# Two graph layers, second layer: an eighth unit by seven products, and two `lo` parts kept in DRAM

## What is computed

```python
def _L0_gnn_ref(h, adj, W_neigh, b_neigh, W_self, b_self):
    deg = jnp.sum(adj, axis=1, keepdims=True) + 1e-05
    h_neigh = (adj / deg) @ h
    out = h_neigh @ W_neigh.T + b_neigh + h @ W_self.T + b_self
    return jax.nn.relu(out)

def _L1_gnn_ref(x, adj, W, b):
    rowsum = adj.sum(axis=1)
    d_inv_sqrt = jnp.where(rowsum > 0, rowsum ** (-0.5), 0.0)
    support = (d_inv_sqrt[:, None] * adj * d_inv_sqrt[None, :]) @ x
    return jax.nn.relu(support @ W + b)
...
x = _layernorm(x + _L0_gnn_ref(x, adj, ...), axis=-1)
x = _layernorm(x + _L1_gnn_ref(x, adj, L1_gnn_W, L1_gnn_b), axis=-1)
```

## Time and profile before

| | us |
|---|---|
| median of 3 runs (lowest, highest) | 776.36 (775.98, 776.51) |
| profiled execution | 776.1 |
| its span, first to last instruction | 774.4 |
| TensorE busy in it | 766.6 |
| VectorE busy | 720.0 |
| ScalarE busy | 429.5 |
| moved by transfers | 161.09 MB |

### The profile page before, as it was taken

The page is one execution under the profiler, slowest core; times in us unless marked ns, Lnnn a source line. Parts: engine busy times, 40 slices in busy tenths (PEclk is TensorE's granted clock), DMA queues, the critical chain, the costliest instruction groups (busy, mean ns, idle before and its releaser), DMA issues.

```text
span 774.4 us, 12666 instructions
## 1 busy us (share of the span) xinstructions
PE 766.6 (99%) x4151; PEld 662.6 (86%) x4151; DVE 720.0 (93%) x1226; ACT 429.5 (55%) x594; POOL 2.5 (0%) x14
## 2 busy tenths in 40 slices
PE   9999999999999999999999999999999999999996
PEld 6888888888888888888888889899898989989896
DVE  6999999999899899998989899898989989898996
ACT  5644645646446364454554755665565566656663
POOL 0000000000000000000000000000000000000000
PEclk9999999999999999999999999999999999999999
DMA  7975574655646547474574756656565665756651
GB/s 302 346 237 195 191 264 155 243 187 200 234 154 244 189 168 266 135 267 168 176 260 147 243 178 208 216 195 241 172 228 198 215 217 176 257 165 229 204 190 61
DMA packets 54206, 161.09 MB, mean 208 GB/s; under 512 B 5024, under 2 KB 18080, under 8 KB 54176
## 3 DMA queue, kind: packets, MB, share of 16 engines
q1 hardware_dynamic: 45680, 151.54, 55.9%
q10 hardware_dynamic: 8352, 9.05, 3.7%
q0 software_dynamic: 144, 0.13, 0.2%
HBM read 152.31 MB, written 8.39 MB: 208 GB/s over the span
## 4 chain that ended last, share of the span: by engine, by line
PE 98%; DVE 1%; ACT 1%; issue 0%; ACTq 0%
PE ps_main L1100 72%; PE ps_epi L979 7%; PE ps_epi L1047 7%; PE ps_main L1038 4%; PE ps_main L1047 2%; PE ps_epi L1038 2%; PE ps_main L979 1%; PE ps_main L1075 1%; PE ps_main L1122 1%; PE ps_main L1060 1%; PE ps_epi L1132 0%; ACT hi L359 0%; ACT xt_sb L382 0%; ACT tt L406 0%; DVE tt L618 0%; PE ps_epi L1000 0%
## 5 line engine op out<-in xcount | busy, mean ns | idle before, releaser
L359 ACT ACTIVATE hi<-raw 128x1024 fp32r<-128x1024 f32 x254 | 254.9, 1013 | 134.5 <-PE ps_main L1100 86.9
L562 DVE TENSOR_TENSOR lo<-raw,hi 128x1024 fp32r<-128x1024 f32 x254 | 296.7, 1170 | 22.5 <-ACT hi L359 22.0
L1100 PE MATMUL ps_main<-hi,xs 128*128 128x512 f32 x1120 | 278.8, 391 | 0.0
L1100 PEld LDWEIGHTS ps_main<-hi,xs 128*128 128x128 f32 x1120 | 207.4, 188 | 41.7 <-issue 0.5
L1100 PE MATMUL ps_main<-lo,xs 128*128 128x512 f32 x560 | 149.7, 389 | 0.0
L853 DVE TENSOR_TENSOR acc<-acc,raw 128x1024 f32<-128x1024 f32 x112 | 136.4, 1218 | 0.0
L1100 PE MATMUL ps_main<-hi,zs 128*128 128x512 f32 x504 | 125.6, 391 | 0.0
L1100 PEld LDWEIGHTS ps_main<-lo,xs 128*128 128x128 f32 x560 | 105.1, 188 | 21.9
L1100 PEld LDWEIGHTS ps_main<-hi,zs 128*128 128x128 f32 x504 | 92.2, 188 | 17.6
L359 ACT ACTIVATE xs<-acc 128x1024 fp32r<-128x1024 f32 (+1 forms) x52 | 54.6, 1050 | 69.3 <-DVE acc L746 55.8
L1047 PE MATMUL ps_epi<-xs 128*128 128x256 f32 x423 | 69.7, 283 | 0.0
(11 more groups left out here) (158 smaller groups left out, 814.8 us busy)
## 6 DMA issues: line engine op xcount, KB each, us to landing
raw<-adj_t SPq DMA_DIRECT2D x256, 512.0 KB, 3.3
res<-x_nat SPq DMA_DIRECT2D x11, 512.0 KB, 5.3
xt_sb<-xt SPq DMA_DIRECT2D x8, 512.0 KB, 5.1
x_scratch<-tt ACTq DMA_DIRECT2D x8, 512.0 KB, 3.8
res<-x_scratch SPq DMA_DIRECT2D x8, 512.0 KB, 4.8
out<-tt ACTq DMA_DIRECT2D x7, 512.0 KB, 4.9
tt<-x_nat SPq DMA_DIRECT2D x3, 512.0 KB, 4.7
acc<-x_nat ACTq DMA_DIRECT2D x1, 512.0 KB, 5.0
```

The lines of the kernel that those rows point to most:

```text
L359: return act.activation(dst, src, ACT.Copy)
L562: return dve.tensor_tensor(dst, src, hi_part.bitcast(f32), ALU.subtract)
L1100: last = pe.matmul(ps[:, f, :], stationary(layer, part, jt, f), mov[:, slot(u), cols], start=(jt == 0 and i == 0), stop=(jt == JT - 1 and ...
```

## The change

- `SU` gets unit 4, so that blocks 1 to 6 of the second layer have eight units by seven products. The last block keeps the five it had, now in a tuple of its own, `SU_LAST`.
- A unit's place in the rings is counted in its own block's list (`s_place`). The table of t sums grows by two tiles of `xs`, and the third place of the ring moves out of `xs` into the first layer's weights `wn` and `ws`, which the loop of the second layer has no use for.
- The t sums of the last group are now those of two units (12 and 13), as in the other groups.
- First layer, blocks 1 to 6: behind the `adj` loads of units 10 and 14, SP stores `lo` of units 6 and 10 (512 KB each, 12 stores in all). VectorE waits for the store before it writes that slot of `lo` again.
- Second layer, blocks 1 to 6: behind the `adj` loads of units 9 and 13, SP waits for `h_ready` of units 6 and 10 and loads their `lo` from DRAM. TensorE's third pass waits for that load. VectorE does a memset of one column in place of `lo`, which gives the signal that frees `raw`.

```diff
@@ -40,9 +40,12 @@
-SU = (1, 5, 7, 9, 11, 12, 13)
+SU = (1, 4, 5, 7, 9, 11, 12, 13)
+SU_LAST = (1, 5, 7, 9, 11)
 NS = len(SU)
 SRING = 3
+KEPT = (6, 10)
+NK = len(KEPT)
 T_AT = XC + FH
 T_UNITS = (4, 6, 9, 11)
 S_AT = T_AT + 2 * NS
...
+        lo_dram = nc.dram_tensor("lo_scratch", [NB, NK, P, UW], f32, kind="Internal").ap()
...
+        lo_stored = [sem(f"lo_stored{s}") for s in range(RING)]
+        lo_full = [sem(f"lo_full{s}") for s in range(RING)]
...
@@ -192,7 +198,28 @@
                 return ()
-            return tuple(u for u in SU if u < TAIL) if is_last(b) else SU
+            return SU_LAST if is_last(b) else SU
+        def kept(b):
+            return () if isinstance(b, int) else KEPT
+        def kept_in_slot(u):
+            return [v for v in KEPT if slot(v) == slot(u)]
+        def kept_count(b, u):
+            per_block = len(kept_in_slot(u))
+            return (b * per_block + (kept_in_slot(u).index(u) + 1 - per_block)) * 16
+        def lead(v):
+            return 1 if v == 2 else max(v - 2, 0)
+        def s_place(b, u):
+            return by_seven(1, b).index(u)
...
@@ -208,19 +235,22 @@
-            return b * NS + (SU.index(u) - NS)
-            return acc[:, (SU.index(u) + 1 - parity) % 2, :]
-            at = S_AT + SU.index(u) % SRING * 4 + part * 2
+            return b * NS + (s_place(b, u) - NS)
...
+            return acc[:, (s_place(b, u) + NS * (1 - parity)) % 2, :]
...
+            s = s_place(b, u) % SRING
+            if s == SRING - 1:
+                return (wn, ws)[part][:, :, :, :].rearrange("p a k f -> p (a k f)")
+            at = S_AT + s * 4 + part * 2
             return xs[:, at:at + 2].rearrange("p a c f -> p (a c f)")
@@ -301,6 +331,17 @@
                     sp.dma_start(raw[:, slot(u), :], adj_in[b, u]).then_inc(raw_full[slot(u)], 16)
+                    if layer == 0 and u - RING in kept(b):
+                        sp.dma_start(lo_dram[b, KEPT.index(u - RING)], lo[:, slot(u), :].bitcast(f32))\
+                          .then_inc(lo_stored[slot(u)], 16)
+                    if layer == 1 and is_first(b) and u == NU - 1:
+                        for v in KEPT:
+                            sp.wait_ge(lo_stored[slot(v)], len(kept_in_slot(v)) * (NB - 2) * 16)
+                    if layer == 1 and u - RING + 1 in kept(b):
+                        v = u - RING + 1
+                        sp.wait_ge(h_ready, g0 + (v + 1))
+                        sp.dma_start(lo[:, slot(v), :].bitcast(f32), lo_dram[b, KEPT.index(v)])\
+                          .then_inc(lo_full[slot(v)], 16)
...
@@ -732,8 +773,8 @@
-                s1, s2, s3 = [s_sum(parity, u, i) for i in range(3)]
-                if SU.index(u) >= 2:
+                s1, s2, s3 = [s_sum(b, parity, u, i) for i in range(3)]
+                if s_place(b, u) >= 2:
                     dve.wait_ge(sl_ready, g - 1)
...
@@ -821,11 +862,18 @@
                         dve.wait_ge(h_ready, g0 + (u + 1))
                         cols = slice(0, UW - HB if u in by_seven(layer, b) else UW)
-                        split_lo(lo[:, slot(u), cols], raw[:, slot(u), cols], hi[:, slot(u), cols]).then_inc(l_ready, 1)
+                        if layer == 0 and u - RING in kept(b):
+                            dve.wait_ge(lo_stored[slot(u)], kept_count(b, u - RING))
+                        if layer == 1 and u in kept(b):
+                            dve.memset(marks[:, 2:3], 0.0).then_inc(l_ready, 1)
+                        else:
+                            split_lo(lo[:, slot(u), cols], raw[:, slot(u), cols], hi[:, slot(u), cols])\
+                                .then_inc(l_ready, 1)
                     place(u, 1)
                     if by_seven(layer, b):
-                        ahead = [v for v in by_seven(layer, b) if max(v - 2, 0) == u]
-                        slot_taken = u in SU and u + 1 in SU
+                        units = by_seven(layer, b)
+                        ahead = [v for v in units if lead(v) == u]
+                        slot_taken = ahead and len([v for v in units if u <= v < ahead[0]]) == 2
                         if ahead and not slot_taken:
                             s_sums(b, parity, ahead[0])
                         if u in by_seven(layer, b):
...
@@ -1092,7 +1140,9 @@
-                        if i == 2:
+                        if i == 2 and layer == 1 and u in kept(b):
+                            pe.wait_ge(lo_full[slot(u)], kept_count(b, u))
+                        elif i == 2:
                             pe.wait_ge(l_ready, g0 + (u + 1))
```

More of the change, by code:

```diff
@@ L209, in s_index, with s_sums_of, s_sum, s_part @@
         def s_index(b, u):
-            return b * NS + (SU.index(u) - NS)
-        def s_sums_of(parity, u):
-            return acc[:, (SU.index(u) + 1 - parity) % 2, :]
-        def s_sum(parity, u, i):
-            return s_sums_of(parity, u)[:, i * HB:(i + 1) * HB]
-        def s_part(part, u):
-            at = S_AT + SU.index(u) % SRING * 4 + part * 2
+            return b * NS + (s_place(b, u) - NS)
+        def s_sums_of(b, parity, u):
+            return acc[:, (s_place(b, u) + NS * (1 - parity)) % 2, :]
+        def s_sum(b, parity, u, i):
+            return s_sums_of(b, parity, u)[:, i * HB:(i + 1) * HB]
+        def s_part(part, b, u):
+            s = s_place(b, u) % SRING
+            if s == SRING - 1:
+                return (wn, ws)[part][:, :, :, :].rearrange("p a k f -> p (a k f)")
+            at = S_AT + s * 4 + part * 2
             return xs[:, at:at + 2].rearrange("p a c f -> p (a c f)")
@@ L392, in s_hi @@
                 act.wait_ge(s_ready, s_index(b, u) + 1)
-                split_hi(s_part(0, u), s_sums_of(parity, u)).then_inc(sh_ready, 1)
+                split_hi(s_part(0, b, u), s_sums_of(b, parity, u)).then_inc(sh_ready, 1)
             def square_tiles(layer, e, parity, pair):
@@ L745, in s_last_sum @@
                 dve.wait_ge(s_chain, s_index(b, u) * 3 + 3)
-                dve.tensor_tensor(s_sum(parity, u, 3), raw[:, slot(u), 0:HB], s_sum(parity, u, 1), ALU.subtract)\
+                dve.tensor_tensor(s_sum(b, parity, u, 3), raw[:, slot(u), 0:HB], s_sum(b, parity, u, 1), ALU.subtract)\
                     .then_inc(s_ready, 1)
@@ L750, in s_lo @@
                 dve.wait_ge(sh_ready, s_index(b, u) + 1)
-                split_lo(s_part(1, u), s_sums_of(parity, u), s_part(0, u)).then_inc(sl_ready, 1)
+                split_lo(s_part(1, b, u), s_sums_of(b, parity, u), s_part(0, b, u)).then_inc(sl_ready, 1)
             def epilogue(layer, e, parity, v, p):
@@ L1044, in seven_products @@
                         pe.wait_ge(sl_ready, s + 1)
-                    mov = s_part((0, 0, 1)[i], u)
+                    mov = s_part((0, 0, 1)[i], b, u)
                     for n, (ps, st, at) in enumerate(summed):
```

## The result

| | before | after |
|---|---|---|
| median, first comparison (3 more runs of before taken beside it) | 776.38 (775.98 to 776.91) | 779.62 (778.27 to 780.30) |
| ratio, 95% interval | | 1.0040 (1.0027 to 1.0053) |
| median, second comparison | 776.81 (776.37 to 778.48) | 779.34 (779.03 to 779.91) |
| ratio, 95% interval | | 1.0031 (1.0019 to 1.0043) |
| profiled execution, its span | 776.1, 774.4 | 780.3, 777.9 |

The change makes the kernel slower, by 2.5 to 3.2 us. The forecast was +1.6 (778.0), with a range to 779.6; the first median (779.62) lies on its upper edge, the second (779.34) inside it. About half of the measured amount was forecast by the first comparison, two thirds by the second.

The account below looks back on a forecast made before the run. TensorE was taken to set the time, with VectorE slightly slower in the second-layer loop and living on a lead. Terms -1.4 + 1.2 + 1.6 + 0.2 = +1.6 us on the median 776.36 gave 778.0 us, range 776.2 to 779.6.

Parts of the forecast that it names:

- unit 4 on TensorE: Second layer, blocks 1 to 6: seven products save TensorE 0.24 us a block, -1.4 us in all.
- wide last group, block 0: Block 0, unit 10: t sums and `t_lo` of a pair delay VectorE, and TensorE's unit 14 waits: +1.6 us, once.
- first-layer stores: Twelve 512 KB stores of `lo` in the first layer, covered by 10 us of room: nothing paid.
- VectorE's list, a block: Blocks 1 to 6: VectorE's added and removed operations balance, 0.0 us a block (-0.2 to +0.1).
- stalls in the loop: Blocks 1 to 6: +1.2 us once VectorE's 1.4 us lead is gone, and +0.2 us for reading `lo` back.
- signs named for the trace: Unit 14 waits 1.6 us; periods 44.9, then 45.4; split waits in blocks 3 to 6; `lo` loads under 5.3, unwaited.
- VectorE's debt: From block 1 to block 6 VectorE loses 2.65 us against a lead of 1.4, costing +1.2 us (0.3 to 2.2).
- The read-back: Loads of `lo` for units 6 and 10: room 5.3 us by block 6, landing 4.2 to 5.0, +0.2 us (0 to 2.0).
- Rival C: The read-back is late, deciding from 5.3 us to landing: at 6.4 us 779.1, at 7.5 us 780.2; chance 0.13.
- rival A: VectorE's lead holds in the loop as waits on ScalarE shrink; only block 0's stall stays: 776.6 us; chance 0.16.
- Rival B: Neither stall, the pair of t sums in block 0 being hidden too: 775.0 us; chance 0.07.
- Rival D: VectorE slower than summed, by register steps and waits: 0.1 us a block is +0.6, 778.6 us; chance 0.10.

Follow-up runs that it names:

- five traces: Traces of kernels with unit 4 and two kept `lo`: changed kernel twice, first t-sum group earlier (779.26 us), first two groups earlier (777.61), last block's residual load moved (779.39).
- the second trace: The changed kernel run again with no edit, for another trace: 779.34 us, ratio 1.0031 against the kernel before.
- one kept unit and none: Changed kernel with `lo` of unit 10 alone stored and loaded (785.09 us, ratio 1.0111), and with no `lo` stored or loaded (791.15 us, 1.0188).
- the three kernels without unit 4: Kernel before; kernel before with only the wide last t-sum group (778.26 us); changed kernel without unit 4 by seven products, last group single (776.92 us).
- three kept units: Changed kernel with `lo` of unit 8 kept as well: 776.79 us, ratio 0.9999; with the first two t-sum groups also a unit earlier: 775.32 us, 0.9979.
- the three kernels without kept `lo`: Kernel before; kernel before with only the wide last t-sum group (778.26 us); changed kernel with no `lo` stored or loaded (791.15 us).
- the kernel with the kept `lo` alone: Changed kernel without unit 4 by seven products, last t-sum group single, stores and loads of `lo` left in: 776.92 us, ratio 1.0001.

## Why the prediction was right in sign and half to two thirds of the size

**Which term went wrong.** By the traces, with what the experiments isolate:

| term | forecast | measured |
|---|---|---|
| unit 4 on TensorE | -1.4 | -1.32 |
| wide last group, block 0 | +1.6 | +1.57 |
| first-layer stores | 0 | 0 |
| VectorE's list, a block | 0.0 (-0.2 to +0.1) | -0.14 (45.38 to 45.24) |
| stalls in the loop | +1.2 and +0.2 | 1.25 and 2.15 (five traces: 1.25 to 2.25) |
| block 7 to the end | 0, not in the sum | +0.4 to +1.2 |

(Stalls in the loop are its length less 269.40; before's 45.38 is from 451.62 in block 1 to 723.87 in block 7, and its end.) Most signs named for the trace came: the weight load for unit 14 waits for the z operation, `join_columns` is 5.09 us behind in block 1 (5.1 forecast), the first three periods are 44.9, the waits on splits come from the middle of the loop on. Two did not: the last period is 44.96 and 45.97 in the two traces and not 45.4, and TensorE waits for loads of `lo`. The Trainium skill's estimate ("TensorE: Matmul & The Clock Gate", Back-to-back issue gap), 0.30 us a block for unit 4, is above the 0.22 measured; the rows were the better source.

**The step that failed: the sum ended with block 6.** VectorE's debt was followed to the end of the loop and its price called 1.2; behind the loop the prediction has no term. But the room there was next to nothing: in the kernel before the last `adj` load was issued at 747.53 and took 5.6 us, so it landed some 0.3 before `hi` of unit 15 ran at 753.37. That row was to be had. In the changed kernel the load goes out at 750.34 and lands after 6.5 us, at 756.9. Counted from the start of block 7 that is an issue 0.5 later (29.51 against 29.03) and a landing 1.0 longer; less the room, it is the 1.2 us. The debt is the smaller part: in the second trace the load even goes out 0.2 earlier than in the kernel before (28.8), and the end is still 0.6 longer, all of it by the landing of 6.6. Only with one kept unit and none is the debt most of it: there the load goes out 1.0 and 1.4 later.

The two loads, each as the view of its line in a narrow window has it (us from issue to landing below), before and then after:

```profile
L303 SPq DMA_DIRECT2D raw<-adj_t x1: 413/413/413, 747.5 to 747.5; - x1
...
DMA to landing us min/median/max: 5.6/5.6/5.6
```

```profile
L333 SPq DMA_DIRECT2D raw<-adj_t x1: 413/413/413, 750.3 to 750.3; - x1
...
DMA to landing us min/median/max: 6.5/6.5/6.5
```

**The read-back was priced at 0.2 and cost 0.5 to 1.9.** Both of the prediction's figures were short. The room was nearly right in block 1, where the load of unit 10 went out at 474.68 and 471.9 + 2.4 for the later block start is 474.3. By the time that it counts it was 4.9 us for a forecast of 5.3: in block 6 of the second trace the load goes out at 701.18 and TensorE is ready at 706.05, and over the thirteen such waits of five traces the room is 4.8 to 5.1. The landing took 4.1 to 5.3 us in the first trace and up to 5.7 in the second, against 4.2 to 5.0 of the residual load that I had taken as the nearest row. So in the first trace every load kept under the limit of 5.3, and TensorE waited 0.5 for one of them all the same. Rival C had this as its condition ("decides from 5.3 us"). It seems too simple in one point: I added its price to the stall on VectorE. In the five traces of kernels with two kept units the waits on VectorE's splits are 0.5 to 1.1 us, not 1.2, and those on loads 0.5 to 1.9; the two traces with the most on loads (1.8 and 1.9) have the least on splits (0.5 each). While TensorE waits for a load, VectorE can catch up. That the two stand in place of one another is a reading of these five traces; no run separates them.

That the range held the result was luck in part: its upper end was drawn for a late read-back and not for the end of the kernel, and in the first trace 0.8 us more came by chance in the first layer.

**VectorE's pace.** VectorE's waits on ScalarE did not shrink with TensorE's shorter blocks (against rival A): 16.3 us in the changed kernel, 16.0 before for `hi`, and 1.6 and 1.5 for the `xs` splits, which the prediction does not count. That added work does not go into them either is shown by the kernels with one kept unit and none: 785.0 and 791.0 were forecast from it, 785.09 and 791.15 came. Rival B fell with block 0. Rival D fell too: the measured pace is 0.14 a block better than before, not 0.1 worse. The one-column memset is busy 0.06.

**What stays open** is why the last `adj` load takes longer in the changed kernel. It landed after 6.4 to 6.6 us in four traces with unit 4 and two kept units and 6.0 in the fifth, 6.2 with one kept unit and with none, 5.6 and 5.8 with three, and 5.2 to 5.6 in the three kernels without unit 4. So the kept `lo` is not the cause. The traces point at one packet of instructions. In the view of transfers, by queue (packets, MB, share of 16 engines), the changed kernel has it from 749.3 to 757 us, while the load is in flight; the kernel before has it only behind the load's landing at 753.1, in the window from 753 to 756:

```profile
q8 instruction: 1, 0.02, 0.7%
```

```profile
q8 instruction: 1, 0.02, 2.0%
```

Either share is about 0.9 to 1.0 us of one engine. Narrow windows place the packet's start at 752.4, which is 2.1 us behind the load's issue, and at 754.4. What the last 0.9 us of the load's own packets look like in the kernel before (751.9 to 752.8) and in the changed one (755.6 to 756.5):

```profile
q1 hardware_dynamic: 42, 0.12, 33.9%
```

```profile
q1 hardware_dynamic: 6, 0.02, 5.6%
```

In the first more than five of the 16 engines end together. In the second a single engine works off the rest alone, as late as one packet of instructions is long. All twelve traces sort by this. In the seven in which the load takes 6.0 us or more, the packet starts 0.3 to 3.5 us behind the issue. With three kept units it starts only 5.4 and 5.0 us behind it, when the load's packets are all but done, and the load takes 5.8 and 5.6; in the three kernels without unit 4 it comes after the landing. Counted from the start of block 7, the packet comes at 30.4 to 32.4 us in every kernel with unit 4 and at 35.7 to 35.9 without. Why unit 4 brings it forward is not shown, and no run moved the packet alone, so this is the likely cause and not a shown one.

## What to carry to other kernels

An engine that is slower than the limiting one lives on a lead. Its debt must be followed to the last instruction of the program and not to the end of the loop, and at each place where it is due, the room is the smallest of several: its own result, and every transfer that its progress releases. A transfer with no room to spare needs a price for its landing too, not only for its issue: here the landing took 5.2 to 6.6 us for the same 512 KB. Moving work into an idle gap gains only if no fixed point (here a product of the other engine) stands between the gap and the deadline; look for the next wait behind the gap before pricing the move. When a stall names a transfer, ask who let the transfer go.

## What the runs showed of the hardware

- Added transfers lengthen all others a little: the median of the `adj` loads is 3.3 and 3.4 us in the three kernels without kept `lo`, 3.4 with one kept unit, and 3.6 to 3.9 with two or three. A load of `lo` with an `adj` load before and behind it lands after 4.1 to 6.5 us; the length differs from block to block and from run to run by over 1 us. The same loads took longest (median 5.9) in the kernel with the kept `lo` alone, in which nobody waited for them.
- The stores of 512 KB to DRAM in the first layer took 4.3 to 5.0 us in the changed kernel's trace, median 4.8, where the earlier trace rows has 3.8 for the store of the normalised rows; that store itself has 4.8 in the changed kernel. 10 us of room covered it. The Trainium skill ("DMA: Bandwidth & Descriptors", Anatomy of one DMA) warns of slow completions of writes to HBM. The trace shows little of it: the loads of `lo`, of the same size, have a median of 4.6.
- A packet of instructions (0.02 MB) keeps one of the 16 DMA engines busy for 0.9 to 1.1 us while the last `adj` load is in flight, and in the seven traces with it the load landed after 6.0 to 6.6 us for 5.2 to 5.8 in the other five.
- Two executions of one kernel can differ by 0.8 us in the first 50 us, and by 0.9 in where a stall falls, while block 0 takes 48.24 to 48.27 in every trace that has its stall. A difference under 1 us has to be split by place before it says anything.
